# Gathers issued in paced groups, the turned rows on ACT's queue, and a prologue with a third PSUM slot, in a CIN tower on one Trainium2 core

## The chip, the cores and the metric

The kernel runs on one NeuronCore of a Trainium2 chip. The metric is the device time of one execution in microseconds (us), as the median of several runs. The engines that matter are PE (TensorE, matmuls), DVE (VectorE, elementwise products), ACT (ScalarE, copies out of PSUM), POOL (GpSimd, which issues the gathers) and SP (SyncE, which only issues transfers).

## What is computed

```
e  = stack of 24 embedding rows of 16 numbers per sample      # [1024, 24, 16], gathered by ids
x1 = einsum('bfd,bhd,fho->bod', e, e,  W0)                     # [1024, 64, 16]
x2 = einsum('bfd,bhd,fho->bod', e, x1, W1)
x3 = einsum('bfd,bhd,fho->bod', e, x2, W2)
z  = concat(x1.sum(d), x2.sum(d), x3.sum(d), dense)            # [1024, 208]
y  = relu(relu(z @ W_top1 + b1) @ W_top2 + b2) @ W_top3        # [1024, 1]
```

## The kernel before

The batch of 1024 samples is cut into 8 tiles of 128. A tile has 2048 columns (16 d by 128 samples), worked on in two halves of 1024, called h0 and h1. Everything is float32, except that the embedding is carried to PE as three bf16 parts whose sum is the float32 value.

**One item.** Layers 1 and 2 are made of items. For an item DVE multiplies two arrays of 128 rows by 1024 columns into one of six `pairs` buffers, and PE contracts that buffer with a weight (`contract`). PE runs three items behind (`LAG = 3`): in iteration n of its loop it contracts item n-3. Layer 2 has 24 items per tile (12 of each half), in sets of four that share one spread of the embedding in PSUM (`rows`, in `spread[0]` or `spread[1]`), multiplied by `units`, x1 broadcast through DRAM. Layer 1 has 6 items per tile, three of each half; they multiply `common` (the embedding, every field repeated) with `turned` (the fields in turned order), which also comes through DRAM, except in the first tile.

**One step.** `body(i)` of each engine computes layer 2 of tile i and layer 1 of tile i+1, 30 items in an order written out by hand in `Plan`. In a middle step the layer 1 items stand at 12, 14, 16 (h0) and 21, 23, 26 (h1); the others are layer 2, first h0, then h1. PE spreads each set one place ahead of its first item, and the two `common` halves at 4 and 8, in the slot that the set of items 0 to 3, and the set of items 4 to 7, leave. At the places of `SIDE` PE also does one round in the single PSUM bank `misc`, which ACT empties (`take`) before the next round: `xt` (transposes of the next embedding) at 0 and 2, `x2t` at 5 and 7, `gram` at 9, 11, 13, 15, `z3` at 17, `x0t` at 21 (eight activations on ACT). At item 20 DVE splits the embedding two tiles ahead of tile i (four operations, lines 291 to 297).

**The two ways through DRAM.** All of these transfers are issued by SP, in program order. For a half of `common`: two stores to `x0_dram` (line 332), then three loads `turned` (line 344), each of which also waits for the product that last read its buffer. For a half of x1: ACT copies the accumulator (`take_x1`, at three places after the last layer 1 item of that half), two stores to `x1_dram` (line 316), then four broadcasts `units` of 512 KB (line 325), one for each j of the items. Items j = 0 to 3 of h0 open the next step. DVE sums the same accumulator into z1 two places later.

**In ACT's loop** the order within one place n is: x2 copy, side round, common copy, x1 copy.

**Prologue.** POOL issues 24 gathers per tile (line 367) one after another, and holds back only for `emb` being free. DVE splits tile 0 when all its 24 gathers have landed; PE transposes it, spreads both halves of `common` into the two slots, and then spreads one item after another into the same two slots.

**Tail.** After the last item PE and ACT do the last `misc` rounds and the three dense layers.

## Time and profile before

| | |
|---|---|
| median of 3 runs | 455.85 us (454.94 to 456.58) |
| the profiled execution | 455.96 us |
| its span in the trace | 454.1 us |
| PE busy | 373.9 us, 82% |
| DVE busy | 303.0 us, 67% |
| ACT busy | 127.6 us, 28% |
| POOL busy | 196.5 us, 43% |

Busy times are sums over one execution. Matmuls are pipelined, so a busy PE is not a PE at its peak. The span is that of the trace; 1.86 us of the profiled execution's time lie outside it.

### The profile page before, as it was taken

What the parts mean: (1) busy time and instruction counts of PE and PEld (TensorE: products, weight loads), DVE (VectorE), ACT (ScalarE), POOL (GpSimd) and SP (SyncE); (2) the same over time, 40 slices, a digit from 0 to 9 for tenths busy, and PEclk for the clock granted to TensorE, in tenths of its full rate; (3) what the DMA queues carried; (4) which work ended last, traced back from release to release, by engine and by line L of the source; (5) the groups of instructions that cost most, each with busy time, mean ns of one, the idle gap of its engine ahead of it and who ended that gap; (6) DMA issues with size and microseconds to landing.
All of it is one profiled execution on the core that took longest, in us unless ns stands there. A gap on an engine that the chain in (4) does not pass through costs nothing. (4 is left out here: it accounts for less than half of the span.)

```text
span 454.1 us, 6457 instructions
## 1 busy us (share of the span) xinstructions
PE 373.9 (82%) x2436; PEld 140.1 (31%) x2436; DVE 303.0 (67%) x305; ACT 127.6 (28%) x228; POOL 196.5 (43%) x196
## 2 busy tenths in 40 slices
PE   0005957995699899889998998899899998999997
PEld 0002201221134134312441243234333421443554
DVE  1003439887657995899599949994999498991000
ACT  1003000331222333234233333233414241127433
POOL 5777777787777877877707760000000000000000
PEclk9999975996889999999999999999989999999999
DMA  7000088366776787678766776876587558700000
GB/s 205 7 7 7 8 203 199 89 180 173 177 169 184 194 199 172 175 196 201 182 183 184 190 184 193 204 186 190 157 204 190 160 154 208 187 2 0 1 0 0
DMA packets 27203, 64.76 MB, mean 143 GB/s; under 512 B 7247, under 2 KB 10759, under 8 KB 27180
## 3 DMA queue, kind: packets, MB, share of 16 engines
q1 hardware_dynamic: 21036, 62.87, 51.4%
q0 software_dynamic: 6144, 1.59, 3.8%
q8 instruction: 14, 0.23, 0.2%
q14 instruction: 9, 0.07, 0.1%
HBM read 58.06 MB, written 6.38 MB: 142 GB/s over the span
## 5 line engine op out<-in xcount | busy, mean ns | idle before, releaser
L395 DVE TENSOR_TENSOR pairs<-spread,units 128x1024 f32<-128x1024 f32 x192 | 223.3, 1220 | 20.3 <-DMA units<-x_dram 13.1
L367 POOL DMA_INDIRECT emb<-in_tbl,ids_sb x192 | 196.3, 1023 | 74.2 <-issue 57.6
L593 PE MATMUL acc<-pairs,w_sb 128*64 128x512 f32 x768 | 200.3, 624 | 15.7 <-DVE pairs L395 14.6
L395 DVE TENSOR_TENSOR pairs<-turned,common 120x1024 f32<-120x1024 f32 x42 | 51.2, 1220 | 40.9 <-DMA turned<-x_dram 34.4
L593 PEld LDWEIGHTS acc<-pairs,w_sb 128*64 128x64 f32 x768 | 45.4, 139 | 106.9 <-DVE pairs L395 52.9
L593 PE MATMUL acc<-pairs,w 120*64 120x512 f32 x180 | 52.3, 666 | 9.9 <-DVE z L400 5.9
L567 PE MATMUL spread<-x0parts,sel 72*128 72x512 bf16 (+1 forms) x140 | 47.2, 426 | 11.2 <-DVE pairs L395 9.1
L455 ACT ACTIVATE x<-acc 128x512 f32<-128x512 f32 x31 | 18.6, 599 | 117.4 <-PE acc L593 117.4
L610 PE MATMUL misc<-ident_b,parts 128*72 128x128 bf16 x120 | 10.4, 235 | 39.9 <-DVE parts L297 37.0
L468 ACT ACTIVATE x0diag<-misc,mask 128x384 f32<-128x384 f32 x64 | 31.7, 611 | 15.2 <-PE misc L613 15.2
L628 PEld LDWEIGHTS misc<-x0diag,x2t 128*64 128x64 f32 x512 | 26.0, 137 | 18.8 <-issue 16.5
L455 ACT ACTIVATE x0parts<-misc 72x1024 bf16<-72x1024 bf16 x15 | 15.2, 1015 | 50.3 <-PE misc L610 50.3
L567 PEld LDWEIGHTS spread<-x0parts,sel 72*128 72x128 bf16 (+1 forms) x140 | 11.0, 117 | 58.2 <-DVE pairs L395 25.5
L628 PE MATMUL misc<-x0diag,x2t 128*64 128x104 f32 x512 | 28.5, 253 | 0.0
L455 ACT ACTIVATE gram<-misc 128x416 f32<-128x416 f32 x32 | 16.5, 517 | 38.3 <-PE misc L628 35.6
L610 PEld LDWEIGHTS misc<-ident_b,parts 128*72 128x72 bf16 x120 | 7.9, 121 | 52.9 <-issue 48.4
L593 PEld LDWEIGHTS acc<-pairs,w 120*64 120x64 f32 x180 | 10.8, 147 | 34.6 <-DVE pairs L395 16.9
L455 ACT ACTIVATE common<-spread 120x1024 f32<-120x1024 f32 x16 | 16.2, 1022 | 15.2 <-PE spread L567 15.2
L291 DVE CAST parts<-emb 128x384 bf16<-128x384 f32 x8 | 3.8, 477 | 24.9 <-DMA emb<-in_tbl,ids_sb 24.9
L455 ACT ACTIVATE x2t<-misc 128x512 f32<-128x512 f32 x16 | 9.6, 597 | 33.7 <-PE misc L618 33.7
L395 DVE TENSOR_TENSOR pairs<-spread,common 120x1024 f32<-120x1024 f32 x6 | 7.2, 1222 | 12.8 <-PE spread L567 8.4
L727 PE MATMUL spread<-units,wt_sb 128*128 128x512 f32 (+2 forms) x48 | 14.4, 453 | 0.0
(38 smaller groups left out, 143.5 us busy)
## 6 DMA issues: line engine op xcount, KB each, us to landing
units<-x_dram SPq DMA_DIRECT2D x64, 512.0 KB, 7.5
turned<-x_dram SPq DMA_DIRECT2D x42, 480.0 KB
x_dram<-x SPq DMA_DIRECT2D x32, 128.0 KB
emb<-in_tbl,ids_sb POOLq DMA_INDIRECT x192
x_dram<-common SPq DMA_DIRECT2D x14, 96.0 KB
x_dram<-common SPq DMA_DIRECT2D x14, 56.0 KB
w_sb<-in_w SPq DMA_DIRECT2D x2, 384.0 KB
wt_sb<-in_wt SPq DMA_DIRECT2D x1, 512.0 KB, 5.5
```

The lines of the kernel that those rows point to most:

```text
L291: eng.tensor_copy(parts[:, :, 0:F], src).then_inc(split_step, 1)
L367: pool.indirect_dma_start(out=e3[:, f, :], out_offset=None, in_=tables[f], in_offset=bass.IndirectOffsetOnAxis(ap=ids_sb[:, t, f:f + 1], a ...
L395: dve.tensor_tensor(pairs[buf][0:rows, :], source[0:rows, :], other[0:rows, h * HALF:(h + 1) * HALF], ALU.mult).then_inc(pairs_done, 1)
L455: return act.activation(dst, src, ACT.Copy)
L468: last = act.activation(x0diag[:, :, :, b, 0:L2_CHUNKS], x0, ACT.Copy, scale=mask[:, b:b + 1])
L567: last = pe.matmul(spread[ring][0:rows, half * BLK:(half + 1) * BLK], sel[:, first:first + rows], src[:, cols(h, half)], start=True, stop= ...
L593: last = pe.matmul(acc[half * H:(half + 1) * H, :], w, pairs[buf][0:rows, half * BLK:(half + 1) * BLK], start=first, stop=final)
L610: last = pe.transpose(xt_bank(i + 1, r)[:, d * P:(d + 1) * P], parts[:, r * 8 + d, :], ident_b[:, :])
L628: last = pe.matmul(misc[e * H:(e + 1) * H, k * 8 * NC:(k + 1) * 8 * NC], x2t[:, r * GK + k, :], x0diag[:, r * GK + k, e, :, :], start=True ...
L727: last = pe.matmul(bank(o)[:, 0:n], wt2_sb[:, k, m * P:(m + 1) * P], h1(k)[:, at:at + n], start=(k == 0), stop=(k == N1 // P - 1))
```

## The change

The gathers are issued in groups, and each group waits for a product of DVE: tile 1 in two groups of 12, tile 2 in two groups of 12, later tiles in three groups of 8. The first tile is split in two parts, 18 fields when they have landed, then 6. The stores of `common` and the loads `turned` are issued by ACT instead of SP, inside ACT's loop: the two stores right behind the copy, the loads at written places. The stores have one semaphore for each half. The layer 1 items of the middle steps stand at 14, 16, 18, 22, 24, 26 and those of the first step at 20, 21, 22, 24, 25, 26; the side rounds, the splits and the `common` spreads of the first step move too. The prologue spreads in the order common h0, items 0, 1, 2, common h1, items 3, 4, 5, over `spread[0]`, `spread[1]` and `acc2`.

```diff
-SIDE_FIRST = {6: ("xt", 0), 8: ("xt", 1), 22: ("x0t", 0)}
+SIDE_FIRST = {9: ("xt", 0), 11: ("xt", 1), 23: ("x0t", 0)}
-MIDDLE = Plan((12, 14, 16, 21, 23, 26), (4, 8), (0, 1), SIDE, {20: 2})
-FIRST = Plan((17, 19, 21, 24, 25, 26), (10, 13), (1, 0), SIDE_FIRST, {4: 1, 24: 2})
-BEFORE_LAST = Plan((12, 14, 16, 21, 23, 26), (4, 8), (0, 1), SIDE)
+L1_AT = (14, 16, 18, 22, 24, 26)
+MIDDLE = Plan(L1_AT, (4, 8), (0, 1), SIDE, {20: 2})
+FIRST = Plan((20, 21, 22, 24, 25, 26), (13, 16), (0, 1), SIDE_FIRST, {8: 1, 28: 2})
+BEFORE_LAST = Plan(L1_AT, (4, 8), (0, 1), SIDE)
+EARLY = 18
+PACE = 8
+PRO_USES = [("common", 0), 0, 1, 2, ("common", 1), 3, 4, 5]
...
 sync: the loop over tiles
-                for h in range(2):
-                    turn_fields(t, h)
                 for h in range(2):
                     spread_units(t, t % 2, h)
...
 gpsimd: gather(t)
                 for f in range(F):
+                    if t == 1 and f == 0:
+                        pool.wait_ge(split_step, 4)
+                    elif t == 1 and f == F // 2:
+                        pool.wait_ge(pairs_done, PRO)
+                    elif t == 2 and f % (F // 2) == 0:
+                        pool.wait_ge(pairs_done, item(0, 8 + f) + 1)
+                    elif t >= 3 and f % PACE == 0:
+                        pool.wait_ge(pairs_done, item(t - 3, 20 + f // PACE * 10) + 1)
...
 vector: prologue
-            split(dve, 0, 0)
+            dve.wait_ge(early_in, EARLY * 16)
+            split_fields(dve, 0, 0, EARLY, early_split, 0)
+            dve.wait_ge(late_in, (F - EARLY) * 16)
+            split_fields(dve, 0, EARLY, F, split_step, 0)
...
 scalar: new helpers
+            def store_fields(i, h):
+                act.wait_ge(common_done, 2 * (i + 1) + h + 1)
+                for first, rows in ((0, F), (F, X0_ROWS - F)):
+                    act.dma_start(x0_dram[h][first:first + rows, :],
+                                  common[0:rows * J_CHUNK:J_CHUNK, h * HALF:(h + 1) * HALF]).then_inc(x0_stored[h], 16)
+            def turn_fields(i, h, c):
+                if c == 0:
+                    act.wait_ge(x0_stored[h], 32 * (i + 1))
+                if h == 1:
+                    act.wait_ge(pairs_done, item(i, plan(i).items.index(("L1", c, 0, 0))) + 1)
+                elif has_last(i):
+                    act.wait_ge(pairs_done, item(i - 1, MIDDLE.items.index(("L1", c, 0, 1))) + 1)
...
+                act.dma_start(turned[c][:, :], bass.AP(rows.tensor, rows.offset, strides)).then_inc(turned_in[c], 16)
...
 scalar: body, behind the common copy at place n
                                 take_common(spread_number(i, use), spread_slot(i, use), h)
+                                store_fields(i, h)
+                        for c in range(L1_CHUNKS):
+                            if n == plan(i).common_at[0] + 3 + (c > 0):
+                                turn_fields(i, 0, c)
+                            if n == plan(i).items.index(("L1", c, 0, 0)) + 2:
+                                turn_fields(i, 1, c)
...
 tensor: prologue
+            pe.wait_ge(early_split, 4)
...
+            for use in PRO_USES:
+                if use == ("common", 0):
+                    spread_x0(SEL_COMMON, COMMON_ROWS, x0parts[0], 0, spread[0])
+                elif use == ("common", 1):
+                    pe.wait_ge(pairs_done, 1)
+                    spread_x0(SEL_COMMON, COMMON_ROWS, x0parts[0], 1, spread[1])
+                    contract(0, L1_ITEMS[0], 0, 0)
+                else:
...
+                    spread_item(L1_ITEMS[use], x0parts[0], pro_source(use))
+                    if use in (3, 4):
+                        contract(use - 2, L1_ITEMS[use - 2], 0, use - 2)
+            for n in range(LAG, PRO):
+                contract(n, L1_ITEMS[n], 0, n)
```

## Rows read from the trace of the kernel before

**Rows 1.** The page: span, and groups (busy us, mean ns, idle before, releaser).
```profile
span 454.1 us, 6457 instructions
...
L367 POOL DMA_INDIRECT emb<-in_tbl,ids_sb x192 | 196.3, 1023 | 74.2 <-issue 57.6
...
L395 DVE TENSOR_TENSOR pairs<-turned,common 120x1024 f32<-120x1024 f32 x42 | 51.2, 1220 | 40.9 <-DMA turned<-x_dram 34.4
```

**Rows 2.** DVE's timeline: start us, length us, operation, idle before it and releaser.
```profile
138.74 1.23 DVE L395 TENSOR_TENSOR pairs<-turned,common 120x1024 f32<-120x1024 f32 x1 [5.16 <-DMA turned<-x_dram]
...
203.72 8.01 DVE L395 TENSOR_TENSOR pairs<-spread,units 128x1024 f32<-128x1024 f32 x7
...
227.52 1.23 DVE L395 TENSOR_TENSOR pairs<-turned,common 120x1024 f32<-120x1024 f32 x1 [6.15 <-PE acc L593]
...
358.59 1.23 DVE L395 TENSOR_TENSOR pairs<-turned,common 120x1024 f32<-120x1024 f32 x1 [5.83 <-DMA turned<-x_dram]
...
384.18 2.41 DVE L395 TENSOR_TENSOR pairs<-spread,units 128x1024 f32<-128x1024 f32 x2 [0.94 <-DMA units<-x_dram]
```

**Rows 3.** SP's queue, one middle step.
```profile
210.80 2.48 SPq L325 DMA_DIRECT2D units<-x_dram  x4
213.58 1.61 SPq L332 DMA_DIRECT2D x_dram<-common  x2
222.54 2.41 SPq L344 DMA_DIRECT2D turned<-x_dram  x3
...
243.01 2.49 SPq L325 DMA_DIRECT2D units<-x_dram  x4
```

**Rows 4.** PE's timeline, the same step.
```profile
211.86 0.64 PE L567 MATMUL spread<-x0parts,sel 72*120 72x512 bf16 x2
...
221.80 0.88 PE L628 MATMUL misc<-x0diag,x2t 128*64 128x104 f32 x16
222.51 1.03 PE L593 MATMUL acc<-pairs,w_sb 128*64 128x512 f32 x4
223.47 0.61 PE L567 MATMUL spread<-x0parts,sel 72*128 72x512 bf16 x2
224.01 1.08 PE L593 MATMUL acc<-pairs,w_sb 128*64 128x512 f32 x4
...
228.80 1.08 PE L593 MATMUL acc<-pairs,w 120*64 120x512 f32 x4 [0.57 <-DVE pairs L395]
```

**Rows 5.** ACT's timeline, the same step.
```profile
218.62 1.02 ACT L455 ACTIVATE common<-spread 120x1024 f32<-120x1024 f32 x1
220.30 0.52 ACT L455 ACTIVATE gram<-misc 128x416 f32<-128x416 f32 x1 [0.65 <-PE misc L628]
...
235.73 0.60 ACT L455 ACTIVATE x<-acc 128x512 f32<-128x512 f32 x1 [2.41 <-PE acc L593]
237.07 3.96 ACT L468 ACTIVATE x0diag<-misc,mask 128x384 f32<-128x384 f32 x8 [0.74 <-PE misc L613]
```

**Rows 6.** The timeline of the start, all engines.
```profile
40.10 1.96 PE L567 MATMUL spread<-x0parts,sel 72*120 72x512 bf16 x4 [1.17 <-ACT x0parts L455]
...
46.99 1.98 PE L593 MATMUL acc<-pairs,w 120*64 120x512 f32 x4
...
54.90 0.60 ACT L455 ACTIVATE x<-acc 128x512 f32<-128x512 f32 x1 [11.72 <-PE acc L593]
55.53 1.16 SPq L316 DMA_DIRECT2D x_dram<-x  x2
58.48 2.51 SPq L325 DMA_DIRECT2D units<-x_dram  x4
...
69.62 1.22 DVE L395 TENSOR_TENSOR pairs<-spread,units 128x1024 f32<-128x1024 f32 x1 [0.82 <-DMA units<-x_dram]
```

**Rows 7.** PE's timeline in step 1, from common h0 to the same spread.
```profile
121.52 1.10 PE L567 MATMUL spread<-x0parts,sel 72*120 72x512 bf16 x2 [4.02 <-DVE pairs L395]
...
135.81 0.61 PE L567 MATMUL spread<-x0parts,sel 72*128 72x512 bf16 x2
```

More of the change, by code:

```diff
@@ L211, in build_tower @@
         common_done = sem("common_done")
-        x0_stored = sem("x0_stored")
+        x0_stored = [sem(f"x0_stored{h}") for h in range(2)]
         turned_in = [sem(f"turned_in{c}") for c in range(L1_CHUNKS)]
@@ L281, in steps, with pro_source, split_fields @@
             body(TILES - 1, 1)
[L283 to L298 removed]
+        def pro_source(n):
+            return (spread[1], acc2.rearrange("p a c -> p (a c)"), spread[0], acc2.rearrange("p a c -> p (a c)"),
+                    spread[0], spread[1])[n]
+        def split_fields(eng, par, lo, hi, done, base):
+            src = emb[par][:, :].rearrange("p (f d) -> p d f", f=F)[:, :, lo:hi]
+            r = rest[:, :].rearrange("p (d f) -> p d f", f=F)[:, :, lo:hi]
+            part = [parts[:, :, k * F + lo:k * F + hi] for k in range(PARTS)]
+            eng.tensor_copy(part[0], src).then_inc(done, 1)
+            eng.wait_ge(done, base + 1)
+            eng.tensor_tensor(r, src, part[0], ALU.subtract).then_inc(done, 1)
+            eng.wait_ge(done, base + 2)
+            eng.tensor_copy(part[1], r).then_inc(done, 1)
+            eng.wait_ge(done, base + 3)
+            eng.tensor_tensor(part[2], r, part[1], ALU.subtract).then_inc(done, 1)
+        def split(eng, t, par):
+            eng.wait_ge(gathered[par], (t - par) * (8 * F) + par * (16 * F))
+            eng.wait_ge(common_done, 2 * t)
+            split_fields(eng, par, 0, F, split_step, 4 * t)
         block = ctx.enter_context(nc.Block())
@@ L326, in spread_units @@
                         .then_inc(units_in[slot][h][j], 16)
-            def turn_fields(t, h):
-                sp.wait_ge(common_done, 2 * t + h + 1)
-                for first, rows in ((0, F), (F, X0_ROWS - F)):
-                    sp.dma_start(x0_dram[h][first:first + rows, :],
-                                 common[0:rows * J_CHUNK:J_CHUNK, h * HALF:(h + 1) * HALF]).then_inc(x0_stored, 16)
-                sp.wait_ge(x0_stored, 64 * (t - 1) + 32 * (h + 1))
-                for c in range(L1_CHUNKS):
-                    if h == 1:
-                        sp.wait_ge(pairs_done, item(t - 1, plan(t - 1).items.index(("L1", c, 0, 0))) + 1)
-                    elif t >= 2:
-                        sp.wait_ge(pairs_done, item(t - 2, plan(t - 2).items.index(("L1", c, 0, 1))) + 1)
-                    rows = x0_dram[h][c * J_CHUNK:c * J_CHUNK + F, :].rearrange("f (j x) -> f j x", j=1)
-                    steps = [list(d) for d in rows.ap]
-                    steps[1] = [HALF, J_CHUNK]
-                    sp.dma_start(turned[c][:, :], bass.AP(rows.tensor, rows.offset, steps)).then_inc(turned_in[c], 16)
             for h in range(2):
@@ L509, in _ @@
             for h in range(2):
-                take_common(h, h, h)
+                take_common(PRO_USES.index(("common", h)), h, h)
             for h in range(2):
@@ L563, in _, with spread_x0, spread_item @@
         def _(pe):
-            def spread_x0(first, rows, src, h, ring):
+            def spread_x0(first, rows, src, h, dst):
                 for half in range(2):
-                    last = pe.matmul(spread[ring][0:rows, half * BLK:(half + 1) * BLK], sel[:, first:first + rows],
+                    last = pe.matmul(dst[0:rows, half * BLK:(half + 1) * BLK], sel[:, first:first + rows],
                                      src[:, cols(h, half)], start=True, stop=True)
                 last.then_inc(spread_ready, 1)
-            def spread_item(what, x0_next, ring):
+            def spread_item(what, x0_next, dst):
                 _, c, _, h = what
-                spread_x0(SEL_L1 + c * COMMON_ROWS, COMMON_ROWS, x0_next, h, ring)
+                spread_x0(SEL_L1 + c * COMMON_ROWS, COMMON_ROWS, x0_next, h, dst)
             def contract(number, what, tile, buf):
@@ L683, in body @@
                                 pe.wait_ge(misc_free, rounds(i) + last_transpose(i) + 1)
[L684 removed]
+                            spread_x0(SEL_COMMON, COMMON_ROWS, x0parts[1 - slot], use[1], spread[buf])
                         else:
[L686 removed]
+                            spread_x0(SEL_ROWS + use[1] % FIELD_GROUPS * P, P, x0parts[slot], use[1] // FIELD_GROUPS, spread[buf])
                     if n >= LAG:
```

49 lines of the change are left out of this document (17 added, 32 removed).

## The prediction

> **What bounds the kernel now.** I read the page first, then DVE's timeline from step to step, then SP's queue, PE and ACT over one middle step. The page says that DVE waits 34.4 us in all for the turned rows, the longest of its waits behind a transfer once the steps run [rows 1]. DVE's timeline shows the rhythm. Item 12 starts at 138.74 in step 1 and at 358.59 in step 6, five steps later: 219.85 / 5 = 43.97 us per step [rows 2]. Products that don't wait take 1.22 us and follow each other every 1.13 to 1.14 us (seven in 8.01 us). In step 3 item 3 ends at 211.73 (203.72 + 8.01); call the end of item 3 P3. Item 12 starts at 227.52 after 6.15 us of standing. So P3 to item 12 takes 15.8 us, of which 6.15 are a stall, and item 12 to the next P3 takes 43.97 - 15.8 = 28.2 us, which is what DVE's own work needs.
>
> SP's queue says why item 12 is late. The four units of 512 KB leave at 210.80, the stores of common at 213.58, and the loads turned, which wait for these stores, only at 222.54: the stores took some 8 us from the end of their issue, behind 2 MB of units on the same queue [rows 3].
>
> **A second chain has no slack.** x1 of h0 is copied at 235.73 to 236.33 [rows 5], and its units leave at 243.01 [rows 3], with the store between. Unloaded, in the prologue, the store takes 2.95 us (55.53 to 58.48), and the fourth unit is multiplied 11.14 us after the first one's issue, at 69.62, after a wait for it [rows 6]. Before, 243.01 + 11.14 = 254.15, and item 3 began near 254.5. What makes x1 later in the step comes out at items 0 to 3 of the next.
>
> **Part by part.** First the middle steps, by these two chains.
>
> *P3 to item 12 after the change.* Item 12 is now layer 2 of h1. It needs no turned row, but the spread of its set, which PE makes at place 11, behind the common spread and everything between. That stretch of PE runs without a gap in the trace: from 211.86 to 224.01, where the contraction behind the spread starts, with one contraction ahead of it (222.51 to 223.47, 0.96 us) that now comes behind the spread. So 12.15 - 0.96 = 11.2 us, and 11.3 from P3 [rows 2, 4]. The queue change removes the 8 us behind the units, if stores on ACT's queue land in some 3 us, as unloaded stores do [rows 6]; then the loads are ahead of item 14.
>
> *ACT's issues.* Ten DMAs a step move from SP to ACT: four stores, six loads. On SP two stores take 1.61 us and three loads 2.41 us, 0.8 us each [rows 3]. On ACT no row shows one. The bounds are 0 (it costs the engine nothing) and 0.8; I take 0.8, as the nearest row. What is queued behind them is the emptying of misc. ACT copied common h1 from 218.62 and gram 0 from 220.30, and PE began gram 1 at 221.80, 10.1 us after P3 [rows 4, 5]. Now c = 0 is issued before that copy (which so runs from 7.7 to 8.7 after P3), two stores and two loads after it (3.2 us, to 11.9), then gram 0's copy to 12.5. PE's gram 1 and the spread behind it come some 2.5 us later. Item 12 is 11.3 + 2.5 = 13.8 us behind P3, against 15.8. If an issue costs nothing, 11.3.
>
> *Item 12 to the next P3.* Layer 1 of h0 now ends at item 18 instead of 16, so ACT's copy of x1 falls on place 21, where the side round x0t stands ahead of it: eight activations of 3.96 us [rows 5]. And PE enters this stretch late, since item 12 is released by its own spread. In the trace 13.06 us pass from the end of that spread at 224.01 to the start of x0diag at 237.07, with 0.57 of waiting [rows 4, 5]; plus the 0.96 of the contraction moved behind the spread this is 13.45 us of PE's own work. DVE is no help: it reaches the end of item 18 after 8 us. Then x0diag and copy, 3.96 + 0.6 = 4.56, store 2.95, fourth unit 11.14, its product 1.2: 13.45 + 4.56 + 2.95 + 11.14 + 1.2 = 33.3 us, where it was 28.2. The later place alone eats what the shorter wait gives.
>
> *The period* is 13.8 + 33.3 = 47.1 us against 43.97, with issues at nothing 44.6.
>
> *PE's clock.* While items 1 to 3 wait for units, PE has nothing to do between its contraction of item 0 and the common spread at P3, some 4.5 us. Where that happened before (4.02 us idle until 121.52), the spread took 1.10 us instead of 0.64, as at the lower of PE's two levels, 1.2 GHz, in place of 2.4 [rows 4, 7]. From there to the start of the same spread it took 135.81 - 121.52 = 14.3 us, where the other step took 223.47 - 211.86 = 11.6: 2.7 us more [rows 4, 7]. The sum leaves this out, and the upper end takes it in: 6 x 2.7 = 16 us.
>
> *The start.* Only 6 of 24 fields are left to split after the last gather. DVE's 28.2 us above hold 22 products (25.1), so two sums and a split take 3.1 us together; of a split of some 2 us I take 1.2 saved, between 0 and 1.6. Up to contraction 2 PE took 14.8 us (40.10 to 54.90); in the new order seven spreads (two in 1.96 us) and three contractions (1.98) follow each other without a wait, 12.8 us: 2.0 saved [rows 6]. So P3 of the first step (69.62 + 1.2 = 70.8) comes 3.2 us earlier, at 67.6. From there 26 products (29.6) and two splits and two sums (5.8) lead to 103.0, and the waits come on top. Layer 1 of h0 stands at 20, 21, 22; its loads leave ACT only at place 16, behind the copy and stores of common h1, at some 90.2, and the first is there 5.0 us later (222.54 to 227.52 [rows 2, 3]) where DVE is ready at 90.7: 4.4 us, and 0.9 for each of the next two. The loads of h1 wait for these products, and the second for x0diag's 3.96 us too: 3.1 and 0.9. The split at place 28 waits 1.7 for twelve gathers that start only behind item 20. A late spread at item 12, behind the transposes at places 9 and 11, is 1.8. In all 13.7: item 0 of step 1 at 116.7 to 117.1, and four products later P3 at 121.7. Item 12 is then at 135.5 (below), against 138.74 before [rows 2]. These waits are my estimates; the bounds are -3 (the whole gain is kept) and +4.
>
> *Costed at nothing.* The other groups of gathers: 8 gathers have ten products, 11.4 us, for their issue, and POOL needs (196.3 + 57.6) / 192 = 1.3 us for one, 10.6 for eight [rows 1], so they fit with little over. If that cover is gone, the split waits, and behind it the transposes and the next x0parts. SP loses work and gains none: the units and x1 stores no longer stand behind the turned rows.
>
> *The end.* From P3 of step 7 (384.18 + 2.41 = 386.59) to the end of the span 67.5 us, unchanged [rows 1, 2].
>
> **The sum.** 121.7 + 13.8 = 135.5 for item 12 of step 1; five periods of 47.1 are 235.5; then 33.3 to P3 of the last step and 67.5: 471.8 us of span. The profiled execution took 1.86 us more than its span (455.96, and the median is 455.85): 473.7, so 474.
>
> **A rule against the change.** Stores that go out behind 2 MB on SP's queue take 8 us here [rows 3]. The Trainium skill (DMA: Bandwidth & Descriptors, section Issuing engines are not separate DMA queues) says that issuing from several engines only saves sequencer time, as all run on the same 16 engines. The same page (Queues, rings and completion order) says that each engine takes turns between the queues' rings by packets, which speaks for short stores on ACT's ring. No trace here shows two such queues at once, so both stay.
>
> **The rivals.**
> 1. *Stores on ACT's queue land no sooner.* ACT stands at the first load until 8 us after the stores' end (3.5 + 8 = 11.5 after P3), and then come load, common copy, stores, loads, gram 0, gram 1, spread: 0.8 + 1.0 + 1.6 + 1.6 + 0.5 + 0.7 + 0.6 = 6.8, so 18.3. Item 12 of step 1 is then at 121.7 + 18.3 = 140.0 and the period 51.6: 140.0 + 258 + 33.3 + 67.5 = 498.8 of span, 501. For it: the 8 us. Against: they lay in one ring behind the units.
> 2. *An issue costs ACT nothing.* Six times 2.5 us less: 474 - 15 = 459.
> 3. *Faster: DVE's own work sets the second stretch.* That is, x1 behind x0diag still arrives in time, since PE works off its backlog in the gaps and units that no longer share a queue with turned land faster than the 11.14 us. Then it is 28.2 again, with 11.3 in front: period 39.5, and 133.0 + 197.5 + 28.2 + 67.5 = 426 of span, 428. For it: the stall of 6 us per step is real, and DVE has no other work there. Against: the 3.96 us stand in ACT's program ahead of the copy. It decides from a period under (454.1 - 135.5 - 33.3 - 67.5) / 5 = 43.6 us.
> 4. *The clock falls in each step:* 474 + 16 = 490, a stronger form of the forecast.
>
> **How the numbers follow.** Forecast (with 4 as its upper part) 0.58, rival 1 0.08, rival 2 0.16, rival 3 0.18. The range 450 to 490 holds the forecast, the clock and rival 2, and the near part of rival 3. Under 0.3% (1.4 us) is about what a measurement of this kernel can't tell from no change. Faster: rival 3 and a little of rival 2, 0.21. Same: 0.05. Slower: 0.74.
>
> **What the profile would show.** The wait for turned at item 12 gone, and DVE there released by PE's spread, PE's gram 1 by ACT's gram copy: right. On ACT's queue two stores of about 0.8 us each behind each common copy, and gram 0's copy some 4 us later than before. The x1 copy right behind x0diag, and DVE waiting for units at items 1 to 3 of each step: right. If items 0 to 3 run in 4.6 us and item 12 follows P3 within 12 us, the forecast is wrong and rival 3 holds. A load turned that leaves ACT over 10 us after P3 would be rival 1. POOL's spans would reach to about 330 us instead of 280, without a split waiting behind them after the first step.

## The result and the profile after

The changed kernel takes 519.12 us (median of 4 runs, 517.38 to 520.00), the kernel before 456.22 beside it: ratio 1.1367, 95% interval 1.131 to 1.1424. The forecast was 474, the range 450 to 490. Slower was right; the size was not. The profiled execution took 519.12 us, of which 517.2 are its span.

The page of the changed kernel: the span and three groups (busy us, mean ns, idle before, releaser).

```profile
span 517.2 us, 6493 instructions
...
L403 DVE TENSOR_TENSOR pairs<-spread,units 128x1024 f32<-128x1024 f32 x192 | 225.2, 1216 | 93.2 <-PE spread L603 70.5
L375 POOL DMA_INDIRECT emb<-in_tbl,ids_sb x192 | 191.3, 997 | 174.2 <-DVE pairs L403 115.2
...
L403 DVE TENSOR_TENSOR pairs<-turned,common 120x1024 f32<-120x1024 f32 x42 | 51.1, 1218 | 10.8 <-DMA turned<-x_dram 8.2
```

The wait for turned rows fell from 34.4 us [rows 1] to 8.2, as the change intends. In its place DVE waits 70.5 us for PE's spread ahead of its layer 2 products (before, all its products together waited 13.5 for it), and POOL waits 115.2 for DVE's products.

DVE's timeline of the changed kernel: the end of the first step, item 12 of step 1, items 3, 8 and 12 of step 3, item 12 of step 6 and the last item 3. P3 stands for the end of item 3, as in the prediction.

```profile
109.44 1.21 DVE L403 TENSOR_TENSOR pairs<-spread,units 128x1024 f32<-128x1024 f32 x1
120.88 0.48 DVE L305 CAST parts<-emb 128x384 bf16<-128x384 f32 x1 [10.22 <-DMA emb<-in_tbl,ids_sb]
...
146.98 2.35 DVE L403 TENSOR_TENSOR pairs<-spread,units 128x1024 f32<-128x1024 f32 x2 [5.12 <-PE spread L603]
...
234.24 1.23 DVE L403 TENSOR_TENSOR pairs<-spread,units 128x1024 f32<-128x1024 f32 x1 [1.04 <-DMA units<-x_dram]
...
243.37 4.62 DVE L403 TENSOR_TENSOR pairs<-spread,units 128x1024 f32<-128x1024 f32 x4 [2.79 <-PE spread L603]
255.34 2.35 DVE L403 TENSOR_TENSOR pairs<-spread,units 128x1024 f32<-128x1024 f32 x2 [7.36 <-PE spread L603]
...
416.00 2.35 DVE L403 TENSOR_TENSOR pairs<-spread,units 128x1024 f32<-128x1024 f32 x2 [7.71 <-PE spread L603]
...
448.77 1.22 DVE L403 TENSOR_TENSOR pairs<-spread,units 128x1024 f32<-128x1024 f32 x1 [0.84 <-DMA units<-x_dram]
```

Item 12 starts at 146.98 in step 1 and at 416.00 in step 6: 269.02 / 5 = 53.8 us a step, against 43.97 before. In step 3, P3 is 234.24 + 1.23 = 235.47, and item 12 follows 19.9 us later (15.8 before).

| stretch | before | after | difference | predicted after |
|---|---|---|---|---|
| to item 0 of step 0 | 62.97 | 60.13 | -2.8 | |
| to P3 of step 1 | 121.4 | 130.2 | +8.8 in all | 121.7 |
| P3 to item 12, step 1 | 17.3 | 16.8 | -0.5 | 13.8 |
| five periods | 219.9 | 269.0 | +49.2 | 235.5 |
| item 12 to P3, last | 28.0 | 34.0 | +6.0 | 33.3 |
| P3 to the end | 67.5 | 67.2 | -0.3 | 67.5 |

The rows from the second on sum to 63.2 us, the difference of the two spans being 63.1.

### The profile page after: what moved, and what is told of

Its sections match the earlier page's. It is cut to its first block and busy times, and to the rows that moved or that the text cites. A ratio compares the mean times of both kernels' runs of the same rounds, so it can differ in the third digit from the quotient of the medians.

```text
span 517.2 us, 6493 instructions
## 1 busy us (share of the span) xinstructions
PE 405.0 (78%) x2436; PEld 150.3 (29%) x2436; DVE 307.3 (59%) x309; ACT 127.8 (25%) x228; POOL 191.5 (37%) x196
## 3 DMA queue, kind: packets, MB, share of 16 engines
q1 hardware_dynamic: 14596, 40.05, 31.5%
## 5 line engine op out<-in xcount | busy, mean ns | idle before, releaser
L403 DVE TENSOR_TENSOR pairs<-spread,units 128x1024 f32<-128x1024 f32 x192 | 225.2, 1216 | 93.2 <-PE spread L603 70.5
L375 POOL DMA_INDIRECT emb<-in_tbl,ids_sb x192 | 191.3, 997 | 174.2 <-DVE pairs L403 115.2
L629 PE MATMUL acc<-pairs,w_sb 128*64 128x512 f32 x768 | 215.4, 672 | 4.5 <-DVE pairs L403 3.7
L629 PEld LDWEIGHTS acc<-pairs,w_sb 128*64 128x64 f32 x768 | 49.4, 148 | 106.2 <-issue 73.2
L629 PE MATMUL acc<-pairs,w 120*64 120x512 f32 x180 | 54.2, 688 | 14.4 <-DVE z L408 11.4
L603 PE MATMUL spread<-x0parts,sel 72*128 72x512 bf16 (+1 forms) x136 | 48.3, 446 | 18.3 <-DVE pairs L403 17.0
L403 DVE TENSOR_TENSOR pairs<-turned,common 120x1024 f32<-120x1024 f32 x42 | 51.1, 1218 | 10.8 <-DMA turned<-x_dram 8.2
L664 PE MATMUL misc<-x0diag,x2t 128*64 128x104 f32 x512 | 33.2, 279 | 21.8 <-ACT gram L464 21.8
L664 PEld LDWEIGHTS misc<-x0diag,x2t 128*64 128x64 f32 x512 | 29.7, 156 | 45.6 <-ACT gram L464 27.0
L464 ACT ACTIVATE x<-acc 128x512 f32<-128x512 f32 x31 | 18.7, 604 | 95.9 <-PE acc L629 93.8
L646 PEld LDWEIGHTS misc<-ident_b,parts 128*72 128x72 bf16 x120 | 8.4, 127 | 63.4 <-issue 53.5
L305 DVE CAST parts<-emb 128x384 bf16<-128x384 f32 (+2 forms) x9 | 4.0, 441 | 35.0 <-DMA emb<-in_tbl,ids_sb 35.0
L629 PEld LDWEIGHTS acc<-pairs,w 120*64 120x64 f32 x180 | 10.5, 147 | 42.6 <-issue 18.1
L408 DVE TENSOR_REDUCE z<-acc 128x512 f32 (+1 forms) x15 | 10.3, 685 | 7.5 <-ACT x L464 7.5
L771 PE MATMUL spread<-units,wt_sb 128*128 128x512 f32 (+2 forms) x48 | 14.4, 453 | 0.0
```

The source lines that it names most:

```text
L375: pool.indirect_dma_start(out=e3[:, f, :], out_offset=None, in_=tables[f], in_offset=bass.IndirectOffsetOnAxis(ap=ids_sb[:, t, f:f + 1], a ...
L403: dve.tensor_tensor(pairs[buf][0:rows, :], source[0:rows, :], other[0:rows, h * HALF:(h + 1) * HALF], ALU.mult).then_inc(pairs_done, 1)
L408: dve.tensor_reduce(z1[:, bass.ds(tile * 2 + h, 1), :].rearrange("p a (k r) -> p (a k) r", r=8), x1_bank(tile, h)[:, :].rearrange("p (k d ...
L464: return act.activation(dst, src, ACT.Copy)
L603: last = pe.matmul(dst[0:rows, half * BLK:(half + 1) * BLK], sel[:, first:first + rows], src[:, cols(h, half)], start=True, stop=True)
L629: last = pe.matmul(acc[half * H:(half + 1) * H, :], w, pairs[buf][0:rows, half * BLK:(half + 1) * BLK], start=first, stop=final)
```

## Why item 12 is late in a middle step

ACT's timeline of the changed kernel, step 3 (ACTq lines are DMA issues); it answers to [rows 5].

```profile
236.74 1.02 ACT L464 ACTIVATE common<-spread 120x1024 f32<-120x1024 f32 x1 [3.68 <-PE spread L603]
237.79 1.54 ACTq L503 DMA_DIRECT2D x_dram<-common  x2
...
244.88 0.60 ACT L464 ACTIVATE x2t<-misc 128x512 f32<-128x512 f32 x1 [2.89 <-PE misc L654]
246.53 0.81 ACTq L518 DMA_DIRECT2D turned<-x_dram  x1
247.45 1.02 ACT L464 ACTIVATE common<-spread 120x1024 f32<-120x1024 f32 x1 [1.97 <-DVE pairs L403]
248.50 1.52 ACTq L503 DMA_DIRECT2D x_dram<-common  x2
250.23 1.68 ACTq L518 DMA_DIRECT2D turned<-x_dram  x2
252.02 0.52 ACT L464 ACTIVATE gram<-misc 128x416 f32<-128x416 f32 x1 [3.55 <-issue]
...
269.93 3.96 ACT L477 ACTIVATE x0diag<-misc,mask 128x384 f32<-128x384 f32 x8 [3.75 <-PE misc L649]
273.73 0.63 ACT L464 ACTIVATE x<-acc 128x512 f32<-128x512 f32 x1
```

PE's timeline, same step; it answers to [rows 4].

```profile
235.59 1.10 PE L603 MATMUL spread<-x0parts,sel 72*120 72x512 bf16 x2 [2.54 <-DVE pairs L403]
236.63 3.68 PE L629 MATMUL acc<-pairs,w_sb 128*64 128x512 f32 x8
...
244.19 0.66 PE L654 MATMUL misc<-ident,x 128*128 128x128 f32 x4
...
252.59 1.66 PE L664 MATMUL misc<-x0diag,x2t 128*64 128x104 f32 x16 [3.88 <-ACT gram L464]
254.18 1.03 PE L603 MATMUL spread<-x0parts,sel 72*128 72x512 bf16 x2
```

Read it backwards from 255.34. The spread of item 12 ends at 255.2; it stands behind gram 1, which waits for ACT to empty misc; that copy starts at 252.02. Ahead of it on ACT lie the load of c = 0, the common copy, two stores and two loads, 5.5 us from the load's start to the gram copy. The prediction had this chain (5.0 us), and 0.8 us for an issue (measured 0.76 to 0.84). What it lacked is at both ends. The load leaves at 246.53, 11.1 us after P3 instead of 6.9, and from gram 0 to item 12 it is 3.3 us instead of 1.8.

Two things hold the load back, and they overlap. One is the stores, for whose landing it waits in ACT's program. The other is PE's clock: the contractions behind the common spread take 3.68 us where they took 1.94 before, so that the second x2t transpose starts 8.7 us after P3, before 5.7, and ACT is through with its copy at 245.48, 10.0 us after P3. The stores end last, 1.05 us later. Taking away either alone would gain little here: without the stores the load could leave at 10.0, and with PE at full clock it left at 10.2 in e5, below. The granted clock of the window 237 to 241 us was 0.50, that is 1.2 GHz, after PE had stood 2.54 us for DVE, which had waited for units. No experiment takes the clock away by itself, so its share is read from these rows alone.

Step 1 of the changed kernel shows the stores without units beside them: ACT's timeline, then SP's last issue before it, then windows of step 1 and step 3 (PE, PEld, DVE, ACT, POOL busy, granted clock, DMA share, GB/s).

```profile
134.12 1.56 ACTq L503 DMA_DIRECT2D x_dram<-common  x2
...
138.75 0.60 ACT L464 ACTIVATE x2t<-misc 128x512 f32<-128x512 f32 x1 [2.36 <-PE misc L654]
138.92 0.80 ACTq L518 DMA_DIRECT2D turned<-x_dram  x1
```
```profile
120.66 2.47 SPq L345 DMA_DIRECT2D units<-x_dram  x4
```

```profile
132.00:136.00 4.00, 3.94 (x20) 1.29 (x18) 4.00 (x4) 1.56 (x3) 3.04 (x4) 1.00 0.17 32
...
237.00:241.00 4.00, 4.00 (x12) 1.18 (x8) 3.58 (x4) 0.76 (x1) 2.00 (x3) 0.50 1.04 247
```

In step 1 the units had gone out long before (120.66), the DMA share was 0.17, and the load left 3.2 us after the end of the stores' issue (135.68 to 138.92), right behind the second x2t copy in ACT's program: the stores landed within the 3 us or so that I had assumed. In step 3 the units left at 234.74, three microseconds ahead of the stores, and 7.2 us pass (239.33 to 246.53), of which the last 1.05, behind the x2t copy, are the stores' alone. Steps 2 to 6 all show 6.9 to 7.3 us there. Another queue did not save the stores from the 2 MB beside them; e4, below, holds the units back and confirms it.

## The experiments

The runs came in five sets, each beside the kernel before. In one of them (the first four rows) it took 457 us, in the four others 580, one of these on the very chip of the first; so times are compared inside a set only, and single steps of different sets only where no gathers are issued (the reason comes below). Two or three times in a row are two or three sets, each a median of all executions. In the first set the kernel before took 565 us once and 577 to 581 six times, and e2, e3 and e4 scatter by 2 to 3% there; a dash stands where the record has no ratio.

| kernel | us | before in the set | ratio, interval |
|---|---|---|---|
| the kernel before again | 456.56 | 457.16 | 0.999 [0.9949, 1.0032] |
| the changed kernel again | 519.39 | 457.16 | 1.1383 [1.1304, 1.1463] |
| e5, ACT's queue only | 481.89 | 457.16 | 1.0587 [1.0504, 1.067] |
| e6, gathers unpaced | 512.66 | 457.16 | 1.1249 [1.1166, 1.1332] |
| e1, turned on SP | 527.8; 529.1 | 580.5; 580.1 | -; 0.9116 [0.9063, 0.9169] |
| e2, x1 first | 547.15; 549.0; 551.84 | 580.5; 580.1; 580.25 | -; -; 0.953 [0.949, 0.957] |
| e3, loads on SP | 527.23; 530.07 | 580.5; 580.1 | -; 0.913 [0.9098, 0.9162] |
| e4, units held | 524.36; 525.43 | 580.5; 580.1 | -; 0.9078 [0.903, 0.9125] |
| s1, prologue only | 580.7 | 580.25 | 1.0016 [0.9997, 1.0036] |
| s2, order only | 589.95; 590.9 | 580.25; 580.33 | 1.0163 [1.0127, 1.0199]; 1.0143 [1.0097, 1.0189] |
| s3, interleaved | 582.49; 581.75 | 580.25; 580.33 | 1.0028 [1.0004, 1.0051]; 1.0029 [1.0003, 1.0055] |

**before_again, after_again.** No edit; they measure what two builds of the same kernel differ by in one set.

> The kernel before, unchanged, to have its trace beside those of the kernels it is compared with. Next to the first four experiments it took 580.5 us, next to the changed kernel 456.2. Theory A: that is a matter of the chip that a set of runs lands on, and here it takes either time again. If it is near 580, the trace should show waits in which DVE, ACT and PE all start late after a semaphore (the experiments show some of 5 to 10 us with a releaser that the trace doesn't know), more of them while POOL issues gathers. Rival: the time moves from load to load, and the spread of the repeats within this set is as wide as 456 to 580.

> The changed kernel, unchanged, in one set with the kernel before. Where before takes 456, it takes 517 to 521. Where before takes 580, theory A (the same waits, but fewer of them, since gathers are paced) gives 520 to 550, so it is the faster of the two there; the rival (the slower setting costs every kernel the same share) gives 519 x 580 / 456 = 660.

**e1_turn_on_sp.** Stores and loads go back to SP's queue, as in the kernel before; all else as changed (`sp_turn` is a new helper with the same stores and loads; its text is left out).

```diff
+                    sp_turn(t, h, True, True)
...
-                                store_fields(i, h)
...
-                                turn_fields(i, 0, c)
...
-                                turn_fields(i, 1, c)
```

> The changed kernel with the stores of common and the turned loads back on SP, everything else as changed. Theory 1 (ACT's queue: from P3, ACT stands at the first load until 246.53 - 235.47 = 11.1 us, and gram 1 and the spread of item 12 come behind it): item 12 follows P3 by 11.3 to 14 us (the second with PE at its lower clock) instead of 20, so six steps gain 6 to 8 us each, 36 to 48 us, and the time is 470 to 485 us. Rival (the new order of the items and the x1 copy behind x0diag are what costs): 505 us or more, since the stretch from item 12 to the next P3 stays at 34 to 35 us and the loads now come late.

The second set, r1_turn_on_sp:

> Again the changed kernel with the stores of common and the turned loads back on SP, where the kernel before takes 456 to 457 us. ACT's queue alone cost 24.7 us on the kernel before (481.9 against 457.2), 4.1 us a step. Theory 1 (all of ACT's part, the 6 to 8 us by which item 12 comes later than 11.3 to 14 us after P3, is its queue): 470 to 485 us. Rival (the new order makes up most of it, and the queue costs what it cost alone): 519 - 25 = 494 us, to 500 with x1 stores again behind the loads.

**e2_x1_first.** The only edit: in the place where both fall, ACT's copy of x1 (`take_x1`) comes before its side round (x0diag) instead of behind it.

> The changed kernel with one thing moved: ACT copies x1 ahead of the side round of the same place, so not behind x0diag (3.96 us). Theory 1b (x0diag in front of the x1 copy delays the units of h0): item 12 to the next P3 falls from 34.7 to about 31.5 us, six times 3 us, 500 us; if DVE then stands under 4 us for units and PE keeps its clock, up to 2.7 us more per step, 485 us. Rival (the copy is not on the path that ends last in that stretch; DVE's own 28 us and the late spread at item 19 are): under 1 us per step, 513 us or more.

The second and third sets, r2_x1_first and t_x1_first:

> Again the changed kernel with ACT's x1 copy ahead of the side round of its place. Theory 1b: item 12 to the next P3 falls by 3 us, 500 us. Rival: DVE's sum of x1 and the late spread at item 19 set that stretch, under 1 us per step, 513 us or more.

> The changed kernel with ACT's copy of x1 put ahead of its side round (x0diag) in the item where both fall; nothing else. If x0diag ahead of the x1 copy is what lengthens the stretch from item 12 to the next P3, each of the six steps gets 4 us shorter (30.7 instead of 34.7 us, as one trace of this kernel on a slower chip had it): 24 us less, about 495 us where the changed kernel takes 519, ratio to the kernel before 1.085. Rival (the wait for x1 is only replaced by that for the turned loads, so the period stays at 53.8): 517 to 519 us, ratio 1.135.

**e3_loads_on_sp.** The stores stay on ACT (`store_fields`), the loads go to SP (`sp_turn(t, h, False, True)`).

> The changed kernel with the stores on ACT's queue and the turned loads on SP. It parts ACT's wait and its six load issues from the ring that the stores lie in. Theory 1 (what costs is that ACT waits): as the kernel with all on SP, 470 to 485 us, and the loads leave SP about 10.5 us after P3, since stores on ACT's queue still land some 7 us after their issue. Rival (ACT's two store issues of 1.5 us behind each common copy cost as much): 495 us or more.

The second set, r3_loads_on_sp:

> Again the changed kernel with the stores on ACT's queue and the turned loads on SP. Theory 1 (ACT's waiting and its load issues cost, its store issues don't): within 5 us of the kernel with all on SP. Rival: ACT's four store issues, 3.1 us a step, cost half of what its queue costs, 12 us or more above it.

**e4_units_held.** SP holds the units of h1 until the stores of common have landed.

```diff
+                if h == 1 and 1 <= t < TILES - 1:
+                    sp.wait_ge(x0_stored[0], 32 * (t + 1))
```

> The changed kernel, but SP holds the units of h1 (2 MB) back until the stores of common h0 have landed. It measures what the stores on ACT's queue wait for. Theory 2 (they wait for the units' packets, though these are in another queue): the first load leaves ACT about 3 us after the stores' issue ends, instead of 7.2 us; item 12 follows P3 by 14 to 16.5 us instead of 20; 495 to 505 us. Rival (a store to DRAM from ACT's queue takes 7 us by itself): the first load leaves as late as before, units come later still, 519 us or more.

The second set, r4_units_held:

> Again the changed kernel with the units of h1 held back until the stores of common h0 have landed. Theory 2 (the stores wait for the units' packets in the other queue): first load 3 us after the stores' issue instead of 7, item 12 some 14 to 17 us after P3 instead of 20, 495 to 505 us. Rival (a store from ACT's queue takes 7 us by itself): 519 us or more.

**e5_act_queue_only.** The kernel before with the stores and loads on ACT at the same kind of places, with one semaphore for the stores of each half as in the changed kernel; order, prologue and gathers as before.

> The kernel before with the stores of common and the turned loads on ACT's queue and nothing else. Theory 1: ACT stands at the first load until the stores have landed, about 11 us after P3, and issues six loads and four stores of 0.77 us in front of gram 0 and gram 1; the spread of the first set of h1 then comes 19 to 20 us after P3 instead of 12.7, and the period grows from 44 to 48 to 50 us: 30 to 40 us more than before in the same set. Rival (the queue is harmless, the new order is what costs): within 5 us of before, or faster, since stores no longer lie behind the units.

**e6_unpaced.** The changed kernel without the four waits added to `gather`.

> The changed kernel with the gathers issued as before, one after another, held back only by the buffer. Theory 3 (pacing costs one wait, that of the split in the first step, 10.2 us, and nothing in the middle steps): 8 to 10 us less than the changed kernel in the same set, where before takes 456. Where before takes 580, theory A has it lose the advantage of the paced kernel: 30 us or more above the changed kernel. Rival (pacing keeps small transfers away from units and turned rows, so the middle steps need it): periods 1 us longer or more in either case.

**s1_prologue_only, s2_order_only.** The kernel before with one part of the change each. s1 also has the semaphore for each half's stores; s2 is the new order in the middle steps, the line shown and the same places in `BEFORE_LAST`.

```diff
-MIDDLE = Plan((12, 14, 16, 21, 23, 26), (4, 8), (0, 1), SIDE, {20: 2})
+MIDDLE = Plan((14, 16, 18, 22, 24, 26), (4, 8), (0, 1), SIDE, {20: 2})
```

> The kernel before with the new prologue alone: the split of the first tile in two parts, the three PSUM slots and the new order of the first spreads; gathers without pacing, all stores and loads on SP's queue, all later steps as before. Theory (the prologue gains what the first profile after showed, item 0 of step 0 at 60.13 us instead of 62.97, and nothing later waits for anything else): 2.8 us less, ratio 0.994, about 453.5 us where the kernel before takes 456.5. Rival (in the first step the work behind item 0 waits for the gathers of the second tile, which do not come earlier): no change, ratio 1.000.

> The kernel before with the new places of the turned products in the middle steps alone (14, 16, 18, 22, 24, 26 instead of 12, 14, 16, 21, 23, 26), which also puts the x1 copy of ACT behind x0diag's. Theory A (the order is what lengthened the stretch from item 12 to the next P3 from 28.2 to 34.7 us, and the later places of the turned products give back part of it ahead of item 12, whose wait for the turned loads goes): period of a middle step 2 to 4 us longer, so 10 to 25 us above the kernel before, ratio 1.02 to 1.05. Theory B (the order costs only together with ACT's queue, since on SP's queue the turned loads now have two items more of time): period not longer than before, ratio 0.98 to 1.00.

The second set, u1_order_only:

> The kernel before with the new places of the turned products in the middle steps alone (14, 16, 18, 22, 24, 26), which also puts ACT's x1 copy behind x0diag's; on the chip of the last set, where the kernel before takes 580 us, it cost 9.7 us (ratio 1.016). Theory A (order and copy are a loss by themselves, some 4 us a step, part of it given back ahead of item 12): 466 to 481 us where the kernel before takes 456, ratio 1.02 to 1.05. Theory B (they cost only together with ACT's queue): ratio 0.98 to 1.00.

**s3_interleaved.** The new prologue and middle order, everything on SP in the order of its use, x1 copy first, gathers unpaced: a try at beating both.

> A version that takes the changed kernel's prologue and its middle order, but all stores and loads on SP's queue with the small stores of common's rows issued ahead of the second half's units and the loads in the order of their use, the gathers unpaced, the x1 copy ahead of the side round and the first step's order as before. Theory (queue, pacing and the copy order hold the whole loss): below the kernel before, period 42 us instead of 44 and a prologue 2.8 us shorter, 440 to 450 us, ratio 0.965 to 0.985. Rival (the order of the items is a loss by itself, as PE gets gaps in it and drops to 1.2 GHz in the stretch between P3 and item 12): 465 to 480 us, ratio 1.02 to 1.05.

The second set, u2_interleaved:

> The changed kernel's prologue and middle order, with all stores and loads on SP's queue in the order of their use, gathers unpaced, the x1 copy ahead of the side round, the first step's order as before; on the last set's chip it took as long as the kernel before (ratio 1.003). Theory (queue, pacing and the copy order hold the whole loss): 440 to 456 us where the kernel before takes 456, ratio 0.965 to 1.000. Rival (the order of the items is a loss by itself): 465 to 480 us, ratio 1.02 to 1.05.

**What they show, part by part.** In the set of 457 us the kernel before and the changed kernel repeated their times (456.56 and 519.39). The absolute times that were expected of e1 to e4 and of s1 to s3 hold for sets of 457 us; all of these landed in sets of 580, so only their steps can be held against what was expected.

*ACT's queue costs 24.7 us by itself* (e5, 481.89 - 457.16); 30 to 40 were expected. ACT's and DVE's timeline of e5, one step (P3 at 218.91):

```profile
220.78 1.54 ACTq L474 DMA_DIRECT2D x_dram<-common  x2
...
225.40 0.60 ACT L435 ACTIVATE x2t<-misc 128x512 f32<-128x512 f32 x1 [2.37 <-PE misc L625]
229.12 0.81 ACTq L489 DMA_DIRECT2D turned<-x_dram  x1
...
239.63 1.23 DVE L375 TENSOR_TENSOR pairs<-spread,units 128x1024 f32<-128x1024 f32 x1 [4.49 <-PE spread L574]
```

Here PE ran at full clock and ACT was free from 226.00, yet the load left at 229.12: the stores took 6.8 us from the end of their issue (222.32), and ACT stood for them. The load left 10.2 us after P3, on SP's queue before 10.8: the stores land no sooner on ACT's queue, and no later. What is new is that ACT stands for them. The loss isn't ahead of item 12, which here is still a turned product (15.0 us after P3, 15.8 before), but behind it: gram 0 is emptied late, PE stands, and item 13 starts 20.7 us after P3, after a wait of 4.49 for its spread. The Trainium skill (DMA: Bandwidth & Descriptors, Issuing engines are not separate DMA queues) says that several issuing engines only save issue time; these rows agree.

*Order and queue, in steps without gathers.* From item 12 of step 5 to item 12 of step 6 POOL issues nothing in the four kernels below, so there the stretch can be compared between sets. Windows view, in the order s1, order only (second run), e5, e6; columns as above.

```profile
441.60:485.10 43.50, 40.89 (x294) 14.99 (x292) 37.47 (x37) 14.14 (x26) 0.00 (x0) 1.00 0.68 185
```
```profile
442.00:489.40 47.40, 42.89 (x290) 15.66 (x290) 37.96 (x37) 14.01 (x25) 0.00 (x0) 0.93 0.64 172
```
```profile
332.20:379.90 47.70, 41.74 (x288) 15.49 (x288) 37.56 (x36) 14.23 (x25) 0.00 (x0) 0.96 0.63 168
```
```profile
357.50:409.60 52.10, 43.38 (x290) 15.97 (x290) 37.87 (x36) 14.13 (x25) 0.00 (x0) 0.93 0.57 152
```

The order alone lengthens the period by 47.4 - 43.5 = 3.9 us (4.6 in its first run), ACT's queue alone by 47.7 - 44.0 = 3.7 (against the kernel before in its own set, where item 12 starts at 316.0 and 360.0; in s1's set the same work takes 43.5), both by 8.1 (52.1 in e6, which also has the new prologue and first step). The changed kernel has 51.8 in its first trace and 54.3 in its second. In this stretch the two parts add up within the spread of the traces. Theory A of s2 holds for it and theory B falls. In s2's whole time only some 10 us show (ratios 1.016 and 1.014, below theory A's 1.02 to 1.05 and above theory B's 1.00), in a set where the steps with gathers are lengthened by other waits. The order alone was never run where the kernel before takes 457, so its share there is not measured by itself; e6 and e5 of that set differ by 30.8 us, which hold the order, the prologue and the first step's new plan.

DVE's timeline of the order-only kernel, second run, shows where the 3.9 us are: item 12, then items 1 to 3 of the next step.

```profile
441.99 2.36 DVE L395 TENSOR_TENSOR pairs<-spread,units 128x1024 f32<-128x1024 f32 x2 [2.16 <-PE spread L567]
...
469.53 1.22 DVE L395 TENSOR_TENSOR pairs<-spread,units 128x1024 f32<-128x1024 f32 x1 [0.63 <-DMA units<-x_dram]
471.67 1.23 DVE L395 TENSOR_TENSOR pairs<-spread,units 128x1024 f32<-128x1024 f32 x1 [0.92 <-DMA units<-x_dram]
473.71 1.23 DVE L395 TENSOR_TENSOR pairs<-spread,units 128x1024 f32<-128x1024 f32 x1 [0.81 <-DMA units<-x_dram]
```

Item 12 to P3 takes 474.94 - 441.99 = 32.95 us (28.2 in s1, 33.3 predicted), P3 to item 12 14.4 (15.3 in s1).

*All kernels in one step.* From P3 of step 6 to P3 of step 7 no kernel of any set issues a gather (the last one ends at 401.7 us, in e2), and DVE has no late start of the kind told below. Several numbers are several traces.

| kernel, step 6 | P3 to item 12, us | item 12 to P3 of step 7, us |
|---|---|---|
| before | 15.5, 15.1 | 28.0, 27.3 |
| s1, prologue only | 15.3 | 26.1 |
| s2, order only | 14.3, 14.4 | 32.2, 33.2 |
| e5, ACT's queue only | 14.4 | 31.5 |
| changed | 18.7, 18.9 | 34.0, 34.3 |
| e6, unpaced | 18.6 | 34.0 |
| e1, turned on SP | 13.2, 14.2 | 32.2, 32.3 |
| e3, loads on SP | 13.2, 14.4 | 32.6, 33.2 |
| e2, x1 first | 18.3, 18.6, 19.1 | 30.3, 30.8, 30.8 |
| e4, units held | 16.7, 15.3 | 35.0, 33.4 |
| s3, interleaved | 11.6, 11.6 | 30.5, 30.5 |

Putting the stores and loads back on SP (e1) takes 5 us off the first stretch and 2 off the second, and leaves about what the order costs alone. The load leaves ACT 10.3 and 10.5 us after P3 in the changed kernel, and SP 11.9 and 10.8 us after it in e1, so no sooner; what went is ACT's standing for it ahead of the gram copies. e3 is the same as e1 inside the measurement, as its theory has it: the stores' issues on ACT cost next to nothing, the waiting and the loads do. The x1 copy first (e2) takes some 3.5 us off the second stretch, as expected of it: the copy behind x0diag is that much of the 6 to 7 us by which the stretch grew. What e2 did to the whole time beside the changed kernel can't be said, since the two never ran in one set. In e4 the first stretch is 2 to 3.5 us shorter. In its step 3 the load left 252.72 - 247.96 = 4.8 us after the stores' issue, at once behind the start of the x2t copy, so the stores had landed by then. The rival, that a store from ACT's queue takes 7 us by itself, falls with this and with step 1 of the changed kernel.

*Pacing costs 6.7 us of the whole* (519.39 - 512.66), where 8 to 10 were expected. In the two traces, which lie 10.7 us apart, item 0 of step 1 starts at 117.2 in e6 and at 126.5 in the changed kernel beside it, since the split's wait for gathers is gone in e6. Step 1 then gives back 2.9 ahead of item 12, and the five periods to item 12 of step 6 take 53.4 us each in e6 and 54.4 in the changed kernel (53.8 in its first trace). The middle steps may cost up to 1 us each for it, which is about what two traces of one kernel differ by; the rival, that they need the pacing, falls.

*The candidate s3* has a period of 44.0 us, and P3 to item 12 in 11.6, but item 12 of step 5 to the next P3 still takes 32.5. In the rows there DVE waits 2.2 us for a unit and 0.9 each for two products with turned rows. It beats nothing: 1.003. The theory's 42 us were not reached; nor does the rival's loss by the order alone stay in the whole time once the x1 copy is first. *s1* gains nothing either (1.002): in its set item 0 of step 0 comes at 113.1 us with the new prologue and at 112.9 without it (s2). The 2.8 us that the new prologue is worth in the first profile could not be tested there.

**What the pacing is good for.** In the sets with 580 us every kernel that paces its gathers took 524 to 552 us (nine medians of four kernels), every one that does not (before, s1, s2, s3) 580 to 591. The start of s1, POOL's and then DVE's timeline:

```profile
92.96 0.95 POOL L388 DMA_INDIRECT emb<-in_tbl,ids_sb  x1 [0.30 <-issue]
123.88 0.95 POOL L388 DMA_INDIRECT emb<-in_tbl,ids_sb  x1 [29.97 <-DVE parts L311]
```
```profile
66.94 1.23 DVE L416 TENSOR_TENSOR pairs<-spread,common 120x1024 f32<-120x1024 f32 x1 [30.49 <-remote]
72.53 1.23 DVE L416 TENSOR_TENSOR pairs<-acc,common 120x1024 f32<-120x1024 f32 x1 [4.37 <-remote]
78.13 1.23 DVE L416 TENSOR_TENSOR pairs<-spread,common 120x1024 f32<-120x1024 f32 x1 [4.38 <-remote]
99.84 1.23 DVE L416 TENSOR_TENSOR pairs<-acc,common 120x1024 f32<-120x1024 f32 x1 [20.48 <-remote]
```

POOL issues gathers without a gap from 3.4 to 93.9 us. From some 38 us on, the other engines start many microseconds after the work that they wait for has ended ("remote" is a releaser that the trace can't name). ACT, for one, copies at 55.66 what PE had transposed by 38.48. Item 0 comes at 113.1 instead of 60 to 63. The changed kernel with one edit (third run of e2) has the same prologue, but its POOL pauses from 33.9 to 36.7 us; ACT makes that copy at 40.23 and DVE the first product at 43.50, although POOL is then issuing its next group. DVE's waits for "remote" are 53.5 us in it and 118.9 in s1. In the sets with 457 us the same unpaced stream shows none of these late starts. The changed kernel itself was not run in a set of the slower kind, nor was e6, so a gain there is argued from e1 to e4, not shown. Nor do these part the pacing from the rest of the change, though no kernel without pacing shows the gain. Which condition of the machine makes the difference stays open; it is not the chip, as one chip showed both, so theory A of before_again falls in that point. Its rival falls too: inside that set all its times lay within 452 to 460 us.

## Why the prediction was wrong

**Right.** The sign; the wait for turned gone at item 12, DVE there released by PE's spread and PE by ACT's gram copy; the issues on ACT at 0.8 us; the second chain: item 12 to P3 was put at 33.3 us and took 34.0 in the last step, 34.7 in step 2 to 3 (200.76 to 235.47), and 32.95 with the order alone; the stall at items 20 to 22 of the first step (4.57, 0.97 and 0.98 us, predicted 4.4 and 0.9 twice); the end, 67.2.

**Wrong, step "P3 to item 12 after the change".** Put at 13.8 us, it took 16.8 in step 1 and 19.9 in step 3. The premise that failed is that "stores on ACT's queue land in some 3 us, as unloaded stores do". They did so in step 1, where they were unloaded (3.2 us at most); in steps 2 to 6, with the units beside them, the load left 6.9 to 7.3 us after their issue, and ACT stood for it. The prediction had ACT send that load 6.9 us after P3; it left at 11.1 in step 3, and at 10.2 in e5 with PE at full clock. In step 1 the load leaves at 8.8, since PE begins the common spread 2.2 us behind P3; the rest of the chain is 1.1 longer.

**Wrong, step "PE's clock".** The fall was foreseen, priced at 2.7 us a step and left out of the sum. In step 3 it costs 3.0 up to the second transpose, nearly all of it beside the wait for the stores, and some 1.5 behind gram 0, where PE had stood 3.88 us for ACT. Rivals 1 and 4 were weighed as alternatives with 0.08 for the first. But the forecast itself contained the waits for units that let PE stand, and the clock did fall in steps 2 to 6; and rival 1's sign, a load that leaves over 10 us after P3, was there in each of them (10.2 to 11.1). Together the two are 501 + 16 = 517, and that this meets 519 is luck: of the 18 us between rival 1's 501 and the measured time 8.5 are the late start, which neither has, and the clock's price is for the most part hidden behind the stores.

**Wrong, step "The start".** P3 of step 1 was put at 121.7 and came at 130.2, outside the bound of +4. The split waited 10.22 us for gathers instead of 1.7. The prediction let the split begin some 16 us after item 20, near 112 by its numbers, with every gather at the mean of [rows 1] and no time for landing. POOL's timeline of the changed kernel shows five of the twelve at up to twice their usual time:

```profile
98.42 0.94 POOL L375 DMA_INDIRECT emb<-in_tbl,ids_sb  x1 [4.64 <-DVE pairs L403]
99.67 1.50 POOL L375 DMA_INDIRECT emb<-in_tbl,ids_sb  x1 [0.30 <-issue]
101.47 1.91 POOL L375 DMA_INDIRECT emb<-in_tbl,ids_sb  x1 [0.31 <-issue]
103.68 1.96 POOL L375 DMA_INDIRECT emb<-in_tbl,ids_sb  x1 [0.30 <-issue]
```

Two more, at 105.94 and 107.96, took 1.72 and 1.78. The five together are 4.2 us over the usual 0.94. Of the 8.5 us, some 2 are that item 20 itself ended later (98.15, where the prediction's numbers give 96.3); 3 that the twelve gathers took 19.1 us instead of 15.9; and over 3 that the last one, issued by 117.24, must land before the split, which begins at 120.88. The step had not priced the last.

In numbers, item 12 of step 6 was put at 135.5 + 235.5 = 371.0 and came at 416.0. Of the 45.0 us, 8.5 are the start, 3.0 P3 to item 12 in step 1, and 5 x 6.7 = 33.5 the periods. Of these 33.5, 28.3 lie between P3 and item 12 and 5.2 between item 12 and the next P3.

## What to carry to other kernels

Moving a dependent load behind its own store onto a compute engine's queue puts the store's landing time into that engine's program; here the store landed no sooner while 2 MB on another queue kept the DMA engines full (share 1.04 in the window of step 3). When a schedule lets an engine stand, cost its clock in the sum and not in the upper end, and don't treat two rivals as alternatives when one causes what the other needs. Check for each reordered producer (here x1) how much slack its consumer had: the 3.96 us of x0diag ahead of the x1 copy cost some 3.5 us a step.

## What was unexpected of the hardware

**Gathers slow down beside DVE's turned products.** A gather's issue on POOL takes 0.94 us; beside products with both inputs in SBUF (`turned`, `common`; DVE runs them at 99.12, 101.33, 103.61, 105.61 and 107.70) the five gathers told of above take 1.50 to 1.96. In the whole trace of the changed kernel every gather that shares 0.9 us or more with such a product takes 1.72 to 1.97; of those that share less, some are longer and some stay at 0.94. Beside products that read `spread` from PSUM it stays at 0.94 to 0.95 (83 gathers). That the sharing of SBUF is the cause is argued, not tested. The Trainium skill (GPSIMD Engine Reference, Specifications) tells of SBUF access shared between POOL and DVE when DVE reads two SBUF inputs; the rows agree.

**One chip ran the same kernel in 457 and in 580 us.** In the slower condition engines start late while POOL issues a long stream of gathers. The kernels with pauses in the stream, which carry the rest of the change too, took 5 to 9% less there than the kernel before.
